# A gated cross- and self-attention block: the row stage transfers two tiles of 128 rows at a time, and its set-up moves into the last cross batch

## The reference, cut to what matters

```python
x = x + tanh(g_xattn) * cross_attention(layernorm(x), ctx)   # 32 x 100 rows of 512, 16 heads of 32, 722 keys
x = x + tanh(g_ffn)   * gated_self_attention(layernorm(x))
# in cross_attention: scores = softmax(q k^T); concat(scores v) @ wo + bo
# in gated_self_attention: qkv = x @ W_qkv; sim = mean over heads of cos(q, g_info), scaled by its min and max
# over all rows; rows with sim > 0.9 and the rest attend only to their own kind
```

## Time and profile before

| | before |
|---|---|
| median of 3 runs | 2761.03 us (2760.5 to 2762.95) |
| profiled execution, its own time | 2773.05 us |
| its span | 2771.2 us |
| PE busy | 2619.4 us, 95%, 17376 matmuls |
| DVE busy | 1819.4 us, 66% |
| ACT busy | 1334.0 us, 48% |
| POOL busy | 379.0 us, 14% |
| stages, from the start of the span | queries to 111, cross to 1992, rows to 2389, self to the end |

### The profile page before, as it was taken

One profiled execution on the slowest core, in us unless ns is written; L12 is line 12 of the kernel. 1 busy time (PEld: TensorE's weight loads), 2 busy tenths in 40 slices (PEclk: granted clock), 3 DMA queues, 4 the chain that ended last, 5 costly groups with the idle time before them and its releaser, 6 DMA issues. The chain is left out here.

```text
span 2771.2 us, 48090 instructions
## 1 busy us (share of the span) xinstructions
PE 2619.4 (95%) x17376; PEld 2346.5 (85%) x17376; DVE 1819.4 (66%) x2867; ACT 1334.0 (48%) x2995; POOL 379.0 (14%) x276
## 2 busy tenths in 40 slices
PE   7899999999999999999999999999679999499999
PEld 7888999989999889998899988999557777388887
DVE  7477666776666776667766677666666666336665
ACT  3344555445554455554455544555333443245554
POOL 0311111111111111111111111111033333000000
PEclk9999999999999999999999999999889999659999
DMA  7654455544445444545444554454379999878983
GB/s 221 197 126 108 121 123 120 128 113 123 120 119 125 120 123 112 125 123 125 119 111 124 124 124 109 120 124 114 83 165 184 188 195 182 152 156 180 194 185 79
DMA packets 368044, 379.89 MB, mean 137 GB/s; under 512 B 128076, under 2 KB 275436, under 8 KB 367852
## 3 DMA queue, kind: packets, MB, share of 16 engines
q1 hardware_dynamic: 316732, 357.13, 55.3%
q10 hardware_dynamic: 51120, 20.11, 3.5%
HBM read 162.57 MB, written 72.57 MB: 85 GB/s over the span
## 5 line engine op out<-in xcount | busy, mean ns | idle before, releaser
L686 DVE TENSOR_TENSOR c_parted<-c_prob,c_parted 128x600 fp32r<-128x600 f32 x512 | 401.0, 783 | 429.2 <-ACT c_prob L629 429.1
L625 ACT ACTIVATE c_parted<-c_pair 128x600 fp32r<-128x600 f32 x512 | 343.9, 672 | 345.2 <-PE c_pair L763 345.1
L672 DVE TENSOR_REDUCE c_peak<-c_pair 100x1 f32<-100x724 f32 x512 | 450.4, 906 | 33.1 <-PE c_pair L745 21.7
L763 PE MATMUL c_pair<-c_q_stack,c_k_stack 100*128 100x100 f32 (+1 forms) x3072 | 381.7, 261 | 0.0
L763 PEld LDWEIGHTS c_pair<-c_q_stack,c_k_stack 100*128 100x128 f32 (+1 forms) x3072 | 369.3, 185 | 4.0
L777 PE MATMUL c_mix<-c_parted,c_v 128*66 128x200 f32 (+1 forms) x3072 | 369.7, 256 | 1.5 <-DVE c_parted L686 0.8
L607 ACT ACTIVATE c_v<-c_work 128x512 fp32r<-128x512 f32 x192 | 115.6, 602 | 481.6 <-PE c_work L91 481.6
L629 ACT ACTIVATE c_prob<-c_pair 128x600 f32<-128x600 f32 x512 | 341.0, 666 | 0.0
L777 PEld LDWEIGHTS c_mix<-c_parted,c_v 128*66 128x66 f32 (+1 forms) x3072 | 323.1, 137 | 13.9 <-DVE c_q_stack L677 0.8
L745 PE MATMUL c_pair<-c_k_stack,c_q_stack 96*100 96x362 f32 x1024 | 259.1, 334 | 3.9
L1453 ACT ACTIVATE s_prob<-s_scores,s_shift 106x100 f32<-106x100 f32 x512 | 169.7, 364 | 142.1 <-DVE s_shift L1520 142.1
(11 more groups left out here) (179 smaller groups left out, 5344.4 us busy)
## 6 DMA issues: line engine op xcount, KB each, us to landing
c_k_stack<-c_k_hi SPq DMA_DIRECT2D x1024, 90.2 KB, 2.2
e_stage<-in_ctx SPq DMA_DIRECT2D x32, 1444.0 KB, 6.4
c_k_stack<-c_k_lo SPq DMA_DIRECT2D x512, 90.2 KB, 2.1
c_q_stack<-q_parts ACTq DMA_DIRECT2D x186, 100.0 KB, 3.1
mix_parts<-c_mixed SPq DMA_DIRECT2D x64, 200.0 KB, 3.2
r_parts<-mix_parts SPq DMA_DIRECT2D x50, 256.0 KB, 4.1
s_q_stack<-qk_parts SPq DMA_DIRECT2D x16, 800.0 KB
s_k_stack<-qk_parts SPq DMA_DIRECT2D x16, 800.0 KB
```

The source lines that it names most:

```text
L625: act.activation(parted[i % PR][:, :, 0, :].rearrange("p (a t) s -> p a t s", a=2), logits, ACT.Exp).then_inc(exp_hi_done, 1)
L672: dve.tensor_reduce(peak[:, i:i + 1], pair[i % 2][0:S, :, 0:HALF], AX.XY, ALU.max).then_inc(peak_done, 1)
L686: dve.tensor_tensor(p[:, :, 1, :], prob[i % 2][:], p[:, :, 0, :], ALU.subtract).then_inc(p_lo_done, 1)
L763: last = pe.matmul(pair[i % 2][0:r, t // (CT // 2), col:col + S], k_stack[:, i, t * P:t * P + r], q_stack[:, i, :], start=True, stop=True)
```

## The change

- Row stage: `parts` is two buffers of 256 rows. The mix and the inverses of a pair of tiles are loaded by six DMAs of 1 KB a row (tiles 0 and 1 by six each of 512 B). A pair's load is issued when both tiles that used the buffer before are joined. The high and low parts of queries and keys are two sets of 256 rows; both tiles of a pair write their half, and four DMAs store the pair after its second tile (tile 24, alone in its pair, is stored by four of 512 B a row).
- Last cross batch: the four split pieces become pieces "row" that split wo with the buffers of wk and wv (ACT high, POOL low), and four more after the scores of heads 6 to 9 split the queries' part of W_qkv. The third weight is loaded behind them. The sums of batches 0 to 27 are loaded, inverted (after the scores of head 3) and stored there; those of the last four batches are loaded and inverted in the row stage, and stored behind tile 2.
- SP no longer waits at the end of the cross stage until all stores have landed; it does so behind tile 0 of the row stage.
- Set-up of the row stage: four constants are loaded on ACT's queue, each wait is for its own constant, g_info is prepared between other work, and DVE joins tile 0. Loops of SP and POOL are written out in full.
- w_hi and w_lo of the first two weights live in the buffers of the cross weights.

```diff
 def batch_plan(with_next):
-    plan = [piece for piece in front_plan() if with_next or piece[0] != "split"]
+    plan = [piece if with_next or piece[0] != "split" else ("row", piece[1], 0) for piece in front_plan()]
...
+        elif h == INVERT_AT:
+            plan.append(("invert", 0, 0))
+        elif 0 <= h - ROW_FROM < KT:
+            plan.append(("row", KT + h - ROW_FROM, 0))
...
             sp.wait_ge(ct_lo_done, B * KT)
-            shared.load_wo(sp, wo)
+            shared.load_weights(sp, 0, wo)
             body(B - 2, False)
+            sp.wait_ge(stored, 48 * EARLY * 4)
+            for a in range(EARLY):
+                sp.dma_start(sums[a * H:(a + 1) * H, :], prob_sums[:, a * BLOCK:(a + 1) * BLOCK]).then_inc(sums_in, 16)
+            sp.wait_ge(cross_w.row_lo, KT)
+            shared.load_weights(sp, 1, w_qkv[:, 0:D])
+            sp.wait_ge(sums_done, 1)
+            for a in range(EARLY):
+                sp.dma_start(inverses[:, a * BLOCK:(a + 1) * BLOCK], sums[a * H:(a + 1) * H, :]
+                             ).then_inc(cross_w.inv_stored, 16)
+            sp.wait_ge(cross_w.row_lo, 2 * KT)
+            shared.load_weights(sp, 2, w_qkv[:, D:2 * D])
             store_mix(B - 1)
-            sp.wait_ge(stored, 48 * B)
...
+            pool.wait_ge(ct_lo_done, B * KT)
+            for n in range(2):
+                for k in range(KT):
+                    pool.wait_ge(cross_w.row_hi, n * KT + k + 1)
+                    pool.tensor_tensor(cross_w.lo[n][:, k, :], shared.raw_weights[:, k, :], cross_w.hi[n][:, k, :],
+                                       ALU.subtract).then_inc(cross_w.row_lo, 1)
...
-        parts = m.sb("parts", [P, 3, KT, P])
-        sums = m.sb("sums", [P, H * ROWS // P])
+        parts = [m.sb(f"parts{i}", [P, 3, KT, 2 * P]) for i in range(2)]
+        last_sums = m.sb("last_sums", [H, BLOCK])
...
+            def load_pair(u):
+
+                width = min(2 * P, ROWS - u * 2 * P)
+                rows = slice(u * 2 * P, u * 2 * P + width)
+                load_mix(u % 2, slice(0, width), rows, a_in[u % 2])
+                load_inverses(u % 2, slice(0, width), rows, a_in[u % 2])
+
+            load_mix(0, half(0), slice(0, P), first_in)
+            sp.wait_ge(cross_w.inv_stored, 16 * EARLY)
+            load_inverses(0, half(0), slice(0, P), first_in)
             sp.dma_start(x_rows[:], x[0:P, :]).then_inc(x_in, 16)
+            sp.dma_start(raw[3], w_qkv[:, 2 * D:3 * D].rearrange("(k p) n -> p k n", p=P)).then_inc(w_in, 16)
+            sp.dma_start(guide[:], repeated(g_info[0, 0:1, :], 0, P)).then_inc(guide_in, 16)
+            sp.dma_start(ffn_bias[:], row_of(b_proj, P)).then_inc(ffn_bias_in, 16)
+
+            load_mix(0, half(1), slice(P, 2 * P), a_in[0])
+            load_inverses(0, half(1), slice(P, 2 * P), a_in[0])
+            load_pair(1)
...
             def store_qk(t):
+
+                u = t // 2
+                width = t % 2 * P + P
                 sp.wait_ge(qk_hi_done, 2 * t + 2)
                 sp.wait_ge(qk_lo_done, 2 * t + 2)
                 for n in range(2):
-                    for part, tile in enumerate((qk_hi[n], qk_lo[n])):
+                    for part, tile in enumerate((qk_hi[u % 2][n], qk_lo[u % 2][n])):
                         dst = qk_parts[2 * n + part].rearrange("(k p) n -> p k n", p=P)
-                        sp.dma_start(dst[:, :, bass.ds(t * P, P)], f32(tile[:])).then_inc(qk_stored, 16)
+                        sp.dma_start(dst[:, :, u * 2 * P:u * 2 * P + width], f32(tile[:, :, 0:width])
+                                     ).then_inc(qk_stored[u % 2], 16)
...
             sp.wait_ge(a_joined, 2)
-            load_parts(2)
...
+            load_pair(2)
+            for t in range(TILES):
+                if t and (t - 1) % 2:
                     store_qk(t - 1)
+                if t + 1 < TILES:
+                    store_x1(t + 1)
+                if t + 2 < TILES:
+                    load_x(t + 2)
+                if t % 2 and t + 5 < TILES:
+                    if (t + 5) // 2 == LATE_PAIR:
+                        sp.wait_ge(last_stored, 16)
                     sp.wait_ge(a_joined, t + 3)
+                    load_pair((t + 5) // 2)
                 store_values(t)
+                if t == 0:
+                    sp.wait_ge(cross_w.mix_stored, 48 * B)
+                    sp.dma_start(last_sums[:], prob_sums[:, EARLY * BLOCK:ROWS]).then_inc(sums_in, 16)
+                if t == 2:
+                    sp.wait_ge(sums_done, 1)
+                    sp.dma_start(inverses[:, EARLY * BLOCK:ROWS], last_sums[:]).then_inc(last_stored, 16)
...
-            def split_qk(t, stored_before=True):
-
-                if stored_before:
-                    act.wait_ge(qk_stored, 64 * t)
+            def split_qk(t):
+
+                u = t // 2
+                if t % 2 == 0 and u >= 2:
+                    act.wait_ge(qk_stored[u % 2], 64 * (u // 2))
                 for n, scale in enumerate((-LOGIT_SCALE, 1.0)):
                     act.wait_ge(qk_turned, 2 * t + n + 1)
-                    act.activation(qk_hi[n][:], turned_qk[n][:], ACT.Copy, scale=scale).then_inc(qk_hi_done, 1)
+                    act.activation(qk_hi[u % 2][n][:, :, half(t)], turned_qk[n][:], ACT.Copy, scale=scale).then_inc(qk_hi_done, 1)
...
+            step.done(dve.memset(eps[:], EPS))
+            dve.wait_ge(value_bias_in, 16)
+            join_attn(dve, 0, False)
             split_attn(0)
+            gate_the_bias()
             split_weights(2)
             residual(0, False)
+            guide_squares()
             split_weights(3)
+            unit_guide()
             split_attn(1)
             body(0, 0)
             body(1, 1)
-            for t in range(2, TILES - 2):
+            body(2)
+            invert_last()
+            for t in range(3, TILES - 2):
                 body(t)
```

More of the change, by code:

```diff
@@ L880, in load_inverses @@
-            def load_inverses(t):
+                    src = mix_parts[n].rearrange("(k p) n -> p k n", p=P)[:, :, rows]
+                    sp.dma_start(parts[buf][:, n, :, cols], src).then_inc(landed, 16)
+            def load_inverses(buf, cols, rows, landed):
                 for j in range(HPT):
-                    src = inverses.rearrange("(k a) n -> a k n", a=HPT)[j:j + 1, :, bass.ds(t * P, P)]
-                    sp.dma_start(parts[j * HD:(j + 1) * HD, 2, :, :], repeated(src, 0, HD)).then_inc(a_in, 16)
@@ new lines, in unit_guide @@
+            def unit_guide():
+                dve.wait_ge(act_setup, 3)
+                step.done(dve.reciprocal(guide_norm[:, 2, :], guide_norm[:, 1, :]))
+                step.wait(dve)
+                step.done(dve.tensor_tensor(by_depth(guide_unit[:]), by_head(guide[:]),
+                                            repeated(guide_norm[:, 2, :].unsqueeze(2), 2, HD), ALU.mult))
+                dve.wait_ge(ffn_bias_in, 16)
+                step.done(dve.tensor_scalar(ffn_bias[:], ffn_bias[:], ffn_gate[:], None, ALU.mult))
+                step.wait(dve)
```

252 lines of the change are left out of this document (123 added, 129 removed).

## The result

The kernel after took 2764.53 us (median of 20 runs, 2752.86 to 2782.42) against 2754.02 for the kernel before in the same comparison (20 runs, 2740.45 to 2763.76). The ratio is 1.0044, 95% interval 1.0028 to 1.0061: slower by 0.44%, some 12 us (the two medians differ by 10.5), where 45 us less were forecast. Its profiled execution took 2764.12 us, with a span of 2762.1.

A forecast was written before the change was run, and what follows sets the result against it. The prediction took the DMA queue to set the row stage's pace, at 14.4 us a tile. Its terms, -31.4 - 11.9 - 2.2 + 2.7 - 2.0, gave -44.8 us, so 2716 us, range 2702 to 2745.

The forecast's parts named there:

- (a): Row stage: 1 KB packets replace 512 B ones, queue time falls from 14.4 to 10.0 us a tile, PE sets the pace.
- (b): Row stage: second buffers end POOL's 192 us and ACT's 33.3 us of waits; step 13.97 to 12.6 us, -31.4 us.
- The margin: Row stage: DVE's chain to L1139 has 0.8 us to spare before PE; POOL's join beside it takes some 0.4.
- Rival 2: Row stage: x rows wait behind 2 MB qk bursts, PE waits 1.6 us every second tile; -26.5, 2734 us; chance 0.17.
- (c): Way into the row stage: first projection at 32.1 us instead of 44.0, -11.9 us; no wait for stores, -2.2 us.
- (d): Last cross batch: copies between exponentials +2.2 us and the inverse on DVE +0.5, sum +2.7 us (+0.5 to +5).
- (e): Row stage's end: ACT's last wait for a qk store goes, -2.0 us (0 to -4); late inverses cost nothing.
- Rival 3: Self stage: PE's low-clock stretch grows, making the kernel slower; 2800 us at 200 us more; chance 0.03.

The follow-up runs named there:

- g3: e4 with q and k stored tile by tile in 512 B rows and two buffers each for x rows, values and similarities; ratio 0.9894 to the kernel before.
- g1: e4 with two buffers each for x rows, values and similarities, x loaded a tile earlier; ratio 0.9892 to the kernel before.
- e2: Kernel after, with POOL's join held back until the similarity of the tile before is done; ratio 1.0017 to the kernel before.
- h1: Kernel after, with only two buffers each for x rows, values and similarities added; ratio 0.9980 to the kernel before.
- e3: Kernel after, with SP issuing the 2 MB of qk stores behind x1 and the x rows; ratio 1.0011 to the kernel before.
- e4: Kernel after with the edits of e1, e2 and e3 together, and the last sums' inverse moved within tile 3; ratio 0.9947 to the kernel before.
- h3: g1 with the early inverse in one piece and the qk stores ahead of x1 and x; ratio 0.9976 to the kernel before.
- e1: Kernel after, with the early sums' inverse in eight pieces after heads 2 to 9; ratio 1.0018 to the kernel before.
- g2: e4 with q and k stored tile by tile, 512 B a row, from the same buffers; ratio 0.9994 to the kernel before.

## Why the prediction was wrong

The sum against the second profile of the kernel before: cross end +9.9, the way to the first load -2.1, front -11.8, steps +17.3, row end +2.4, self +3.2, in all +18.9; the spans differ by 18.8. Against the first it is 12.2 - 2.1 - 11.8 + 2.8 + 2.2 - 12.4 = -9.1. The measured +12 lies between the two; single executions of the kernel before differ by 14.5 us in the steps and 15.6 in the self stage.

Most of the miss is in the steps. The forecast had 289.8 us for the 23 and they took 324.0: a calm step of 13.43 in place of 12.6 (some 18 us in 22 steps), the excess of five long ones (12.1) and of the one with the late inverse (4.1). The last cross batch adds 9.5 us to the miss and the end 4.2. And the 321.2 us that the saving was counted from came from one profile: the second has 306.7, and by it a step of 12.6 would have saved 16.9 us and not 31.4.

**(a) Wide transfers.** The step that failed is the inference "that is more than the step, so the queue sets the pace". 14.4 us of packet time a tile didn't set it: g3 has a share of 103.0% and steps of 12.4 (12.8 us of packet time a tile by 1.03 x 12.4). The saving in packet time came in the forecast direction, 14.4 to 11.3 a tile where 10.0 was forecast. With two buffers for all but x1 it bought nothing: g1 and g3 agree. What the pace hung on was when single transfers landed for buffers that had no second. The 52.8 ns a packet that I started from was already a mean over stalls, and not the price of a packet. The queue of the kernel before, from 2133 to 2134 in a burst and from 2142 to 2143 behind it:

```profile
q1 hardware_dynamic: 659, 0.33, 113.7%
q1 hardware_dynamic: 58, 0.03, 75.1%
```

That is 27.6 ns a packet in the burst and 207 behind it, with a share of 75% all the same. In the kernel after, a microsecond of a burst (2119 to 2120) has 387 packets of 1 KB at a share of 109.8%, 45.4 ns each: 0.38 MB in the microsecond against 0.33. I set the rule of the Trainium skill, DMA: Bandwidth & Descriptors, Specifications (line rate from 512 B on) aside on the strength of that mean. By that rule the wide stores gain next to nothing, and g1 against g3 agrees; the loads were not tried narrow.

**(b) Two buffers.** The waits of POOL and ACT went as forecast, and the step of 12.6 was the right floor (12.39 in g1). The margin was too small, as the last paragraph of the prediction has it: of 0.8 us I gave POOL's join 0.4. It costs (1487 - 676) + (1011 - 176) ns = 1.65 us, twice the whole margin, and 1.65 - 0.8 = 0.85 is close to the 0.75 us that PE waits. I had read the slowed L1113 in the earlier trace rows as a mean of +0.4, where the thing to look at is which operations POOL now stands beside. It left two on DVE (L1113 and L1134) and came to two others, and these are ahead of L1203. e2 shows the term in its calm steps, 1.0 us each; over 23 steps that would be 24 us, an estimate, and g1 against h1 comes near it (26.0 us, of which 4.1 are the late inverse).

**Rival 2, the burst,** had its place right (DVE's wait for x rows) and its size roughly: 14.3 us of DVE's waits in six tiles and 12.1 us in five long steps, where I had PE wait 1.6 us in twelve tiles. It was priced as an alternative to the margin being too small; both came. And it is a family rather than one wait: x rows (after, e2), values (e3, e4), similarities (e4), x1 (h3), one behind the other.

**(c) The front**: right, 32.2 us against 32.1 forecast, and -2.1 against -2.2. The agreement to 0.1 is luck: PE starts 12.7 us after the first load (10.5 forecast) and on tile 1's mix after 27.9 (26.9), which then takes 4.3 (5.15); what lies between made up the rest.

**(d) The last cross batch**: +12.2 against +2.7, and outside its bound of +5. The inverse was given 0.5 us because DVE had slack by heads. It had none: PE stood still for 2.41 us (its wait for L729), and the granted clock fell from 1.00 to 0.5 there and stayed so up to 0.8 us before the last result. Counted from the batch's first mix, the kernel after takes 11.8 us more than the kernel before, and e1 and g2, with pieces and a clock of 1.00, 2.8 us more. So the forecast of +2.7 was near for the copies and an inverse that PE doesn't stand still for. The inverse in one piece, given 0.5 us, cost 9 more: its own length as far as PE stood still for it, and the time at the lower clock. How the 9 divide wasn't measured, and what moved ahead of the first mix is not in this count.

**(e) The end**: +2.2 against -2.0. ACT's wait of the earlier trace rows went, but the last stores, which now stand behind 2 MB issued from 2370.41 on, take longer to land. SP's last store and the first load of the self stage, the kernel after:

```profile
2382.03 1.00 SPq L966 DMA_DIRECT2D qk_parts<-r_k_lo  x1
...
2392.76 0.34 SPq L1416 DMA_DIRECT2D s_sim<-sim  x1
```

That is 10.7 us, against 6.6 in the first profile of the kernel before (2382.88 to 2389.46). The late inverses, priced at nothing since they are used so much later, hold DVE for 2.63 us ahead of L1203 at tile 3, and that step took 17.5 us, 4 more than a calm one, also in h1 without the wait for x rows.

**Rival 3** named the clock in the self stage as the way to slower. There the clock did vary, by chance and in the kernel before too. The way to slower was three costs that I had as small or zero: the last cross batch (12 us), the join (1.0 a tile in calm steps) and the single buffers (12 in the five long steps, that with the late inverse, L1173, left out). Against them stood gains that were real for the front and not for the queue.

## What to carry to other kernels

A queue share near 1 didn't mean that the queue set the pace (g3). Before transfers are made cheaper, list every buffer with no second and ask which one a larger burst will make late. The change paid fully (324.0 us of steps to 285.1) only when x rows, values and similarities had a second, x1's store was issued ahead of the burst, and the join was held back. When a wait is removed, look at what the freed engine now runs beside: POOL's instructions held DVE operations, all but one of them with two inputs in SBUF, up until they had ended. And take more than one profile before a mean step is a baseline: two of the same kernel gave 13.97 and 13.33 us.

## What the runs showed that was not expected

In the kernel after, a gap of PE of 2.41 us that ends at 1976.40 came with some 24 us at the lower clock (1975.4 to 1999.2); the same matmul groups of the mix took 0.73 to 0.78 us before it and 1.24 behind it. The length of the gap doesn't settle it: in the row stage of the same trace a gap of 2.28 us that ends at 2095.28 left the clock at 1.00, one as long that ends at 2204.47 was followed by 3 us at 0.50, and in four kernels with the inverse in pieces the clock fell without any such gap. DVE and POOL do not slow each other in proportion: a product of 16 columns, 176 ns alone, took 1011 beside POOL, as it waited for the end of POOL's instruction. And three edits, each of which alone leaves the kernel no faster than the one before (1.0018, 1.0017, 1.0011, against 1.0044 without any), gave 0.9947 together, and 0.9873 to 0.9892 with the second buffers.
